# Gate and up matmuls of 64 experts: 512 moving columns for the high weights, the halves of the result added by ScalarE and DVE

## What is computed

```python
h = jax.nn.silu(jnp.einsum('ech,ehi->eci', inp, wg)) * jnp.einsum('ech,ehi->eci', inp, wu)
out = jnp.einsum('eci,eih->ech', h, wd)
```

## Time and profile before

| | us |
|---|---|
| median of 3 runs | 1830.6 |
| lowest and highest | 1830.03, 1832.79 |
| the profiled execution | 1829.67 |
| its span, first to last instruction | 1827.9 |
| mean granted TensorE clock | 0.996 of full speed |

### The profile page before, as it was taken

How to read it: one execution, slowest core, us unless ns; L and a number is a source line. 1 busy time by engine, 2 the same in 40 slices (tenths; PEclk the granted TensorE clock), 3 DMA queues, 4 the chain that set the end, 5 groups by cost and what they waited for, 6 DMA issues and landing times.

```text
span 1827.9 us, 37431 instructions
## 1 busy us (share of the span) xinstructions
PE 1801.4 (99%) x13303; PEld 1324.2 (72%) x13303; DVE 1441.4 (79%) x2387; ACT 1232.0 (67%) x1799; POOL 1064.1 (58%) x813
## 2 busy tenths in 40 slices
PE   9999998999999999999999999999999999999997
PEld 5666667777777777777777777777777777777775
DVE  5999997787778877778777777777787877777772
ACT  6999996666666666666666666666666666666662
POOL 1101003766677677666666666666677677666651
PEclk9999999999999999999999999999999999999999
DMA  7677764899989999999999999999999999999982
GB/s 248 222 259 248 254 229 166 304 310 308 304 305 310 307 299 298 298 298 297 297 298 297 299 297 302 302 306 307 305 304 308 308 302 296 299 296 298 298 284 46
DMA packets 95818, 516.99 MB, mean 283 GB/s; under 512 B 17697, under 2 KB 22817, under 8 KB 71841
## 3 DMA queue, kind: packets, MB, share of 16 engines
q1 hardware_dynamic: 47968, 357.19, 49.1%
q0 software_dynamic: 42912, 151.04, 35.5%
q10 hardware_dynamic: 4896, 8.26, 1.6%
HBM read 409.21 MB, written 107.22 MB: 283 GB/s over the span
## 4 chain that ended last, share of the span: by engine, by line
PE 93%; DVE 3%; issue 1%; ACT 1%; DMA 0%; POOLq 0%; POOL 0%; DVEq 0%; ACTq 0%
PE ps_gu L549 54%; PE ps_d L563 27%; PE ps_s L426 5%; PE ps_j L415 3%; PE ps_l L446 2%; PE ps_t L438 1%; PE ps_w L464 1%; DVE zb L946 0%; DVE zb L918 0%; PE ps_w L475 0%; DMA xg<-h_rows,table 0%; DVE at L974 0%; PE ps_t L415 0%; DVE split_u L1163 0%; DVE split_g L1158 0%
## 5 line engine op out<-in xcount | busy, mean ns | idle before, releaser
L1329 POOL DMA_INDIRECT xg<-h_rows,g_idx x504 | 724.6, 1438 | 188.1 <-issue 133.1
L549 PE MATMUL ps_gu<-xT,split_g 128*128 128x256 bf16 x4608 | 534.1, 273 | 0.8 <-DVE xT L1218 0.8
L549 PE MATMUL ps_gu<-xT,split_u 128*128 128x256 bf16 x4608 | 534.1, 273 | 0.0
L563 PE MATMUL ps_d<-split_d,act 128*128 128x512 bf16 x2304 | 508.1, 379 | 1.5 <-DVE act L1178 1.3
L549 PEld LDWEIGHTS ps_gu<-xT,split_g 128*128 128x128 bf16 x4608 | 450.8, 98 | 66.6 <-issue 1.1
L549 PEld LDWEIGHTS ps_gu<-xT,split_u 128*128 128x128 bf16 x4608 | 450.9, 98 | 52.1
L563 PEld LDWEIGHTS ps_d<-split_d,act 128*128 128x128 bf16 x2304 | 225.1, 98 | 260.7 <-DVE act L1178 2.6
L835 ACT ACTIVATE ob<-ps_d,wcol 128x512 f32<-128x512 f32 x256 | 173.0, 688 | 337.7 <-PE ps_d L563 302.2
L1349 POOL DMA_INDIRECT out<-ob,s_idx x128 | 205.5, 1606 | 291.7 <-ACT ob L835 241.5
L1168 DVE TENSOR_TENSOR split_d<-raw_d,split_d 128x1536 bf16<-128x1536 f32 x128 | 219.3, 1755 | 93.2 <-ACT split_d L807 93.1
L1184 DVE STREAM_TRANSPOSE xt<-xg 128x512 f32<-128x512 f32 x252 | 163.9, 689 | 130.0 <-DMA xg<-h_rows,g_idx 130.0
(11 more groups left out here) (121 smaller groups left out, 1399.1 us busy)
## 6 DMA issues: line engine op xcount, KB each, us to landing
raw_d<-in_wd SPq DMA_DIRECT2D x63, 1536.0 KB
raw_g<-in_wg SPq DMA_DIRECT2D x62, 1536.0 KB
raw_u<-in_wu SPq DMA_DIRECT2D x62, 1536.0 KB
h_rows<-hrow SPq DMA_DIRECT2D x33, 640.0 KB, 3.4
xb<-in_x SPq DMA_DIRECT2D x32, 512.0 KB, 4.9
out<-xb SPq DMA_DIRECT2D x32, 512.0 KB, 3.6
xg<-h_rows,g_idx POOLq DMA_INDIRECT x504
ctx_sb<-in_ctxT SPq DMA_DIRECT2D x8, 512.0 KB, 6.0
```

Of the source, the lines that this page charges most:

```text
L549: mm = pe.matmul(ps_gu[m][:, t, :], w[:, wi, k, m * P:(m + 1) * P], xT[u][:, k, xi, :], start=(k == 0 and (wi, xi) == (0, 0)), stop=(k == ...
L563: mm = pe.matmul(ps_d[n][:], act[u][:, ai, m, half * P:(half + 1) * P], split_d[:, wi, m, c * NH:(c + 1) * NH], start=(m == 0 and (wi, ai) ...
L1329: p.indirect_dma_start(out=xg[u][:, g, :], out_offset=None, in_=h_rows, in_offset=bass.IndirectOffsetOnAxis(ap=g_idx[u][:, g:g + 1].bitcas ...
```

## The change

For each step k, the high weights are multiplied with the high and low rows together, in one matmul of 512 columns that fills a bank, and the low weights with the high rows in a second matmul of 256 columns that adds to the first half of it. So each of the six products (block m, gate or up) has a bank of its own with two halves that have to be added: the first has high x high and low x high, the second high x low. Five banks ps_gu are used in rotation, bank (2m + t) % 5; the sixth product, up of block 2, takes the bank of gate of block 0 again and waits for gate_summed. Three banks ps_d are used for the four down parts, so part 3 waits for the copy of part 0. ps_x shares its place with the third of them.

For gate, ACT copies the second half to sil (gate_part), DVE adds the first half to it (gate_sum), and ACT's silu then works on sil in place. For up, DVE adds the halves by a reduction over pairs (tensor_reduce of a 128x256x2 view, linked) at the head of activate. gu_done is parted in gate_done and up_done. The new steps are put into the hand-written orders of ACT and DVE. first_turns uses other banks. The declarations of the four semaphores and the loops' count of linked instructions (12 to 18) are left out here.

```diff
@@ -291,9 +294,17 @@
         ps_p = ps("ps_p", [P, E], F32, p_mem)
         p_mem.close()
 
-        ps_gu = [ps(f"ps_gu{m}", [P, 2, CAP], F32, ctx) for m in range(MI)]
-        ps_d = [ps(f"ps_d{i}", [P, NH], F32, ctx) for i in range(4)]
-        ps_x = ps("ps_x", [P, QS, 2, E], F32, ctx)
+        ps_gu = [ps(f"ps_gu{i}", [P, 2, CAP], F32, ctx) for i in range(5)]
+        ps_d = [ps(f"ps_d{i}", [P, NH], F32, ctx) for i in range(2)]
+        x_mem = ExitStack()
+        ps_x = ps("ps_x", [P, QS, 2, E], F32, x_mem)
+        x_mem.close()
+        ps_d.append(ps("ps_d2", [P, NH], F32, ctx))
+
+        def bank(m, t):
+            return ps_gu[(2 * m + t) % 5]
+
+        FIRST_TURNED = [ps_gu[1][:].rearrange("p x c -> p (x c)"), ps_gu[3][:].rearrange("p x c -> p (x c)"), ps_d[0][:], ps_d[1][:]]
 
         block = ctx.enter_context(nc.Block())
 
@@ -537,30 +548,32 @@
 
             def half_gate_up(e, u, m, t, first=False):
                 w = (split_g, split_u)[t][u]
+                out_ps = bank(m, t)
                 if m == 0:
                     pe.wait_ge((g_low, u_low)[t], 2 * e + 2)
+                if m == MI - 1 and t == 1:
+                    pe.wait_ge(gate_summed, MI * e + 1)
                 for k in range(KH):
                     if m == 0 and t == 0 and k % 2 == 0:
                         if first:
                             pe.wait_ge(first_low, k // 2 + 1)
                         else:
                             pe.wait_ge(xT_out, 4 * e + k // 2 - 3)
-                    for wi, xi in PAIRS:
-                        mm = pe.matmul(ps_gu[m][:, t, :], w[:, wi, k, m * P:(m + 1) * P], xT[u][:, k, xi, :],
-                                       start=(k == 0 and (wi, xi) == (0, 0)),
-                                       stop=(k == KH - 1 and (wi, xi) == (1, 0)))
-                return mm
+                    pe.matmul(out_ps[:].rearrange("p x c -> p (x c)"), w[:, 0, k, m * P:(m + 1) * P],
+                              xT[u][:, k].rearrange("p x c -> p (x c)"), start=(k == 0), stop=False)
+                    mm = pe.matmul(out_ps[:, 0], w[:, 1, k, m * P:(m + 1) * P], xT[u][:, k, 0], start=False, stop=(k == KH - 1))
+                mm.then_inc((gate_done, up_done)[t], 1)
 
             def gate_up(e, u, m):
                 pe.wait_ge(act_ready, MI * e - MI + m + 1)
                 half_gate_up(e, u, m, 0)
-                half_gate_up(e, u, m, 1).then_inc(gu_done, 1)
+                half_gate_up(e, u, m, 1)
 
             def down_part(u, n, ms):
                 half, c = n // 2, n % 2
                 for m in ms:
                     for wi, ai in PAIRS:
-                        mm = pe.matmul(ps_d[n][:], act[u][:, ai, m, half * P:(half + 1) * P],
+                        mm = pe.matmul(ps_d[n % 3][:], act[u][:, ai, m, half * P:(half + 1) * P],
                                        split_d[:, wi, m, c * NH:(c + 1) * NH],
                                        start=(m == 0 and (wi, ai) == (0, 0)),
                                        stop=(m == MI - 1 and (wi, ai) == (1, 0)))
@@ -570,16 +583,18 @@
 
                 pe.wait_ge(d_low, 2 * e + 2)
                 pe.wait_ge(act_ready, MI * e + MI - 1)
+                if first:
+                    pe.wait_ge(pieces_made, 1)
                 for n in range(2):
                     if not first:
-                        pe.wait_ge(down_out, 4 * e - 3 + n)
+                        pe.wait_ge(down_out, 4 * e - n)
                     down_part(u, n, range(MI - 1))
                 pe.wait_ge(act_ready, MI * e + MI)
                 for n in range(2):
                     down_part(u, n, [MI - 1]).then_inc(down_done, 1)
                 for n in range(2, 4):
-                    if not first:
-                        pe.wait_ge(down_out, 4 * e - 3 + n)
+                    if n == 3:
+                        pe.wait_ge(down_out, 4 * e + 1)
                     down_part(u, n, range(MI)).then_inc(down_done, 1)
 
             def expert(e, u):
@@ -592,7 +607,7 @@
                 for half in range(2):
                     pe.wait_ge(first_rows[half], 16)
                     for k in range(KH):
-                        mm = pe.transpose(ps_d[k // 2][:, k % 2 * CAP + half * P:k % 2 * CAP + (half + 1) * P],
+                        mm = pe.transpose(FIRST_TURNED[k // 2][:, k % 2 * CAP + half * P:k % 2 * CAP + (half + 1) * P],
                                           xg[0][:, QS * half + k // 2, k % 2 * P:(k % 2 + 1) * P], ident[:])
                         if half:
                             mm.then_inc(first_turned, 1)
@@ -602,7 +617,7 @@
                 for m in range(MI):
                     half_gate_up(0, 0, m, 0, True)
                 for m in range(MI):
-                    half_gate_up(0, 0, m, 1, True).then_inc(gu_done, 1)
+                    half_gate_up(0, 0, m, 1, True)
                 down(0, 0, True)
 
             attention_done(pe)
@@ -788,14 +803,14 @@
             def gate_high(e, u, part, first=False):
                 s.wait_ge(g_loaded[u], 8 * (e - u) + 16 * PARTS * (2 - u))
                 if not first:
-                    s.wait_ge(gu_done, MI * e - MI)
+                    s.wait_ge(gate_done, MI * e - MI)
                 ks = slice(part * KH // 2, (part + 1) * KH // 2)
                 s.activation(split_g[u][:, 0, ks], raw_g[u][:, ks], ACT.Copy).then_inc(g_high, 1)
 
             def up_high(e, u, part, first=False):
                 s.wait_ge(u_loaded[u], 8 * (e - u) + 16 * PARTS * (2 - u))
                 if not first:
-                    s.wait_ge(gu_done, MI * e - MI)
+                    s.wait_ge(up_done, MI * e - MI)
                 ks = slice(part * KH // 2, (part + 1) * KH // 2)
                 s.activation(split_u[u][:, 0, ks], raw_u[u][:, ks], ACT.Copy).then_inc(u_high, 1)
 
@@ -806,9 +821,15 @@
                 cs = slice(part * NH, (part + 1) * NH)
                 s.activation(split_d[:, 0, :, cs], raw_d[:, :, cs], ACT.Copy).then_inc(d_high, 1)
 
+            def gate_part(e, m, first=False):
+                s.wait_ge(gate_done, MI * e + m + 1)
+                if m == 0 and not first:
+                    s.wait_ge(act_ready, MI * e)
+                s.activation(sil[:, m], bank(m, 0)[:, 1], ACT.Copy).then_inc(gate_copied, 1)
+
             def silu(e, m):
-                s.wait_ge(gu_done, MI * e + m + 1)
-                s.activation(sil[:, m], ps_gu[m][:, 0], ACT.Silu, scale=H_SCALE).then_inc(sil_done, 1)
+                s.wait_ge(gate_summed, MI * e + m + 1)
+                s.activation(sil[:, m], sil[:, m], ACT.Silu, scale=H_SCALE).then_inc(sil_done, 1)
 
             def turned_high(e, u, q):
                 s.wait_ge(turned, 4 * e + q - 3)
@@ -816,7 +837,7 @@
 
             def first_high_part(n):
                 s.wait_ge(first_turned, 2 * n + 2)
-                s.activation(xT[0][:, 2 * n:2 * n + 2, 0], ps_d[n][:].rearrange("p (k c) -> p k c", k=2), ACT.Copy
+                s.activation(xT[0][:, 2 * n:2 * n + 2, 0], FIRST_TURNED[n].rearrange("p (k c) -> p k c", k=2), ACT.Copy
                              ).then_inc(first_high, 1)
 
             def weights(e, u):
@@ -832,7 +853,7 @@
                     s.wait_ge(scattered, 32 * e - 32)
                 for n in range(4):
                     s.wait_ge(down_done, 4 * e + n + 1)
-                    s.activation(ob[u][:, n // 2, n % 2 * NH:(n % 2 + 1) * NH], ps_d[n][:], ACT.Copy,
+                    s.activation(ob[u][:, n // 2, n % 2 * NH:(n % 2 + 1) * NH], ps_d[n % 3][:], ACT.Copy,
                                  scale=wcol[u][:, n // 2:n // 2 + 1]).then_inc(down_out, 1)
 
             def expert(e, u, first=False, last=False):
@@ -843,6 +864,7 @@
                 if not last:
                     turned_high(e + 1, 1 - u, 0)
                     turned_high(e + 1, 1 - u, 1)
+                gate_part(e, 0)
                 silu(e, 0)
                 if not last:
                     gate_high(e + 1, 1 - u, 0, none_before)
@@ -850,9 +872,12 @@
                     turned_high(e + 1, 1 - u, 2)
                     turned_high(e + 1, 1 - u, 3)
                     weights(e + 1, 1 - u)
+                gate_part(e, 1)
                 silu(e, 1)
                 if not last:
                     up_high(e + 1, 1 - u, 0, none_before)
+                gate_part(e, 2)
+                if not last:
                     up_high(e + 1, 1 - u, 1, none_before)
                 silu(e, 2)
                 rows_out(e, u, first)
@@ -869,12 +894,15 @@
                 down_high(0, 0, True)
                 down_high(0, 1, True)
                 s.wait_ge(silu_table, 1)
+                gate_part(0, 0, True)
                 gate_high(1, 1, 0, True)
+                gate_part(0, 1, True)
                 gate_high(1, 1, 1, True)
+                silu(0, 0)
+                gate_part(0, 2, True)
                 up_high(1, 1, 0, True)
-                silu(0, 0)
+                silu(0, 1)
                 up_high(1, 1, 1, True)
```

(22 more changed lines are left out.)

5 lines of the change are left out of this document (4 added, 1 removed).

## The result

The changed kernel takes **2092.7 us** (median of 4 runs, 2090.7 to 2095.1) against 1830.3 before (4 runs beside them): the ratio is 1.143, interval 1.142 to 1.145. 2101 was forecast, in a range of 2040 to 2165. The profiled execution took 2093.4 us, its span is 2091.6 us, 263.7 longer than before.

The account below looks back on a forecast made before the run. TensorE, busy 99% of the span, was taken as the bound; waits in the ACT and DVE queues would add 62 x 4.05 + 3.1 = 254 us, the clock 17, together 271 on 1830.6: 2101 us, range 2040 to 2165.

Parts of the forecast that it names:

- The bound and the margins: TensorE bounds, 23.49 us per expert; VectorE's slack is 5.2 us, but act of block 2 has only 0.7 in hand.
- Gain of the form: Gate and up matmuls: 48 of 512 and 48 of 256 columns take 15.60 us, not 15.72; 8 us gained in all.
- dear and cheap reductions: VectorE's reductions: dear, 1.28 us each, +110, 2210 (9%); cheap, near 0.42, within a milder cross-wait under 2020 (8%).
- The schedule step by step: ACT and DVE queues through one expert: TensorE waits 2.8 us for act 1, 1.3 for act 2; expert 27.5 us.
- the 4.05: Added time per expert from both TensorE waits, 27.5 us in place of 23.49, counted for 62 experts.
- no step of VectorE waits for ScalarE in the middle of an expert: Kernel before, VectorE's queue: the reason given for block 1's act having 2.5 us of margin.
- "By the work alone it would fit": VectorE per expert: 3.2 us of sums and reductions raise 18.3 us to 21.5, below 23.4.
- Expert 0: First expert, with its own order: act 2 at 332.2, next expert's first matmul at 337.4 instead of 334.30, +3.1 us.
- "The three down banks cost nothing while ACT is free": Down stage: part 3 waits for part 0's copy, 0.9 us after its end, but stands behind 12 matmuls (2.59 us).
- The clock: TensorE's granted clock falls to 0.50 in some waits, about 2.4 us into a gap or sooner; 0.27 us per expert, 17 us.
- The sum: Whole kernel: 62 x 4.05 + 3.1 = 254 us, plus 17 for the clock, 271, added to the median 1830.6.

Follow-up runs that it names:

- new_order: The changed kernel with both queues reordered: ScalarE's copy of block 1 earlier, VectorE's sums moved, both gate_low behind act 2; about 1897 us.
- form_alone: The changed kernel with only the matmul form and banks, without copies, sums and reductions; 23.37 us per expert, 5 us less than the kernel before.
- work_alone: The kernel before plus three copies, three sums and three linked reductions per expert on a constant tile, nothing waiting for them; period up 1.32 us.
- kept_busy: The changed kernel with ten extra 512-column matmuls on TensorE ahead of the wait before the down stage; median 3.4 us lower.

## Why the prediction was right

- **The bound and the margins.** That the cost would come from where VectorE's slack lies, and not from its sum, held: with the same work in another order (new_order) the change costs 67 us instead of 262.
- **Gain of the form,** 0.12 us: right (form_alone, 23.37 against 23.49). **Durations:** the reduction was taken as 0.69 us; its median in the trace is 683 ns, so dear and cheap reductions are both out. The estimate of 0.66 us by the Trainium skill (VectorE: DVE Perf Modes, the perf-mode tier table and the errata table) was 0.02 low. A copy was 0.37 to 0.39, a sum 0.42.
```profile
L1206 DVE TENSOR_REDUCE prod<-ps_gu x192: 676/683/692, 325.9 to 2072.2; 128x256 f32<-128x512 f32 x192
```
- **The schedule step by step** is the part that carried the number. Forecast and measured, from TensorE's first gate matmul: copy 0 ready to be summed at 5.03 (4.97); act 0's reduction from 8.30 (8.18); turns done at 11.45 (11.33); copy 1 from 12.94 (12.79), sum 1 from 13.32 (13.21); act 1 at 18.39 (18.35); act 2 at 22.31 (22.20). VectorE's two idle stretches were 0.92 and 1.88 us (1.1 and 1.9 forecast), the period 27.50 (27.54, 23.49 + 4.05). The schedule's own end is 22.31 + 5.18 = 27.49, which is 4.00 more than 23.49; the 4.05 that went into the sum is a slip, 3 us in all. That no step of VectorE waits for ScalarE in the middle of an expert was too strong a reading: the earlier trace rows show 1.40 us for the down split and 1.45 us for the last silu, neither of them ahead of block 1. The page puts only 211.8 us on TensorE's wait, not 260: it draws each piece 0.17 us too long, 18 us in all, and in the 21 of 62 experts with a fall of the clock the slower matmuls fill the second wait, 26 us.
- **"By the work alone it would fit"** was too kind: alone it costs 1.3 us per expert (work_alone), since block 2's margin of 0.7 us is smaller than what was put ahead of it. The schedule had counted the work at its place, so the sum was not touched by it.
- **Expert 0:** 3.1 us forecast, 5.7 measured (first intervals 28.13 and 22.41). Up to act 2 the walk held: ready at 332.2 by the forecast, at 334.88 in the trace, in which the experts begin 2.6 us later. What it put at nothing was the third bank. "The three down banks cost nothing while ACT is free": in expert 0 ScalarE isn't free, its copy of part 0 stands behind four turned_high and the weight columns, and TensorE's part 3 waits for it (TensorE, then ScalarE):
```profile
341.14 3.09 PE L576 MATMUL ps_d<-split_d,act 128*128 128x512 bf16 x9 [2.80 <-ACT ob L856]
```
```profile
339.51 0.86 ACT L846 ACTIVATE wcol<-xg 32x2 f32<-32x2 f32 x4
340.40 1.84 ACT L856 ACTIVATE ob<-ps_d,wcol 128x512 f32<-128x512 f32 x3
```
- **The clock** was taken at 17 us; the falls are worth 7.4. The step that each stretch at 0.50 gives back 1.3 us into the second wait held: a raised period is 0.43 us longer (27.85 to 28.0). How often was too high: 21 falls in the 62 periods, 16 of them raised so, and 5 by 0.1 us. The reading that a fall comes about 2.4 us into a gap or sooner did not hold: 5 of the 22 came that early, the others up to 4.1 us after TensorE had stopped. The five early ones are those that raise little, since the first 0.5 to 0.7 us at 0.50 lie in the gap. The Trainium skill (TensorE: Matmul & The Clock Gate, HAM oscillation) describes a loop in which the array waits 3 to 5 us once per pass and the clock falls in every pass; here, with waits of 2.8 us, it fell in 21 of 62, and kept_busy shows that removing the falls hardly pays.
- **The sum:** 62 x 4.00 = 248, expert 0 5.7, clock 7.4, and 2.6 us by which the experts began later: 263.7, the difference of the spans. (The last term is hardly the change's: in work_alone, which has the banks and matmuls of the kernel before, they begin 2.5 us later too.) Forecast: 251 + 3 + 17 = 271. The number came out 0.4% high because the clock's 9.6 us and the slip's 3 too much outweigh 2.6 too little for expert 0 and 2.6 that nobody forecast; that they partly cancel is luck, the 248 is not.

## What to carry to other kernels

Slack of an engine says whether new work fits; only a walk through its queue, instruction by instruction against the bounding engine's clock, says whether it fits where it is put. Here this walk was right to 0.2 us for the changed kernel and wrong by 1.2 us per expert for new_order, where a signal came late that no row had shown, and for expert 0 it left out one wait on a bank. So walk each order of the queue that differs, and run a new order before counting on it. When a result has to pass from one engine to another and back (copy, sum, activation), put each half of the exchange ahead of work that waits for something else, and put work that nobody needs yet behind the result that somebody does: moving one copy was worth 132 us here, moving two splits 190. Look also at what a change can win at best before paying for it: the form alone gives 5 us, and with the work that it needs the best order tried was 11 us slower than the kernel before.

## What the runs showed of the hardware that was not expected

- In new_order the signal of an expert's last up matmul is recorded 0.01 us after its end in some experts and mostly 1.4 to 1.7 us after it in others of the same execution, and VectorE's reduction starts 0.02 us behind it. With ScalarE's experts written out, 10 of 64 reductions are over 1.3 us late; with them in a loop, 59. Of the eight experts written out on VectorE 6 are still late, of TensorE's 7. The cause was not found.
- The granted clock fell to 0.50 for 3.41 us each time, 2.1 to 4.1 us after TensorE had stopped for a gap of 2.8 us. It fell in five groups of four consecutive experts, with none in the six or seven between, and once in each of experts 0 and 2. The falls of a group start 27.31 us apart and its gaps end 27.8 to 28.0 apart, so each fall comes earlier against its gap: the first 1.2 to 1.35 us after TensorE had resumed, the second 0.6 to 0.7, the third within 0.1 us of it, and the fourth 0.5 to 0.7 us before it. A fourth one, in a gap from 691.6 to 694.25 (columns as above):
```profile
693.00:693.60 0.60, 0.00 (x0) 0.00 (x0) 0.56 (x2) 0.00 (x0) 0.57 (x2) 1.00 1.11 464
693.80:694.20 0.40, 0.00 (x0) 0.00 (x0) 0.40 (x2) 0.00 (x0) 0.00 (x0) 0.50 1.36 571
```
